# Adding a mixing bias to x on VectorE instead of through four small-K TensorE products a group

## What is computed

```python
att   = softmax(mlp(cond_128))                      # 64 x 8
agg_w = einsum('bk,koi->boi', att, weight)          # a 32x32 channel mixer per batch
agg_b = att @ bias_k                                # 64 x 32: one number per batch and channel
m     = einsum('boi,bih->boh', agg_w, x) + agg_b[:, :, None]
gate  = top-2 softmax over 8 experts of m @ gate_w.T
x1    = x + m @ base_w.T + base_b + 2.0 * (lora experts of m, weighted by gate)
out   = x1 + second layer (9-tap grouped convolution of x1, top-2 of 4 lora experts)
```

## Time and profile before

| | |
|---|---|
| median of 3 runs | 185.46 us (184.99 to 186.48) |
| profiled execution, its device time | 185.67 us |
| profiled execution, its span | 183.7 us |
| busy over the span | PE 96%, DVE 65%, POOL 46%, ACT 45% |
| granted TensorE clock | 1.0 in the mean |

### The profile page before, as it was taken

One profiled execution on the slowest core, in us unless ns is written; L12 is line 12 of the kernel. 1 busy time (PEld: TensorE's weight loads), 2 busy tenths in 40 slices (PEclk: granted clock), 3 DMA queues, 4 the chain that ended last, 5 costly groups with the idle time before them and its releaser, 6 DMA issues.

```text
span 183.7 us, 3003 instructions
## 1 busy us (share of the span) xinstructions
PE 176.0 (96%) x1087; PEld 160.1 (87%) x1087; DVE 119.6 (65%) x255; ACT 82.9 (45%) x183; POOL 84.2 (46%) x86
## 2 busy tenths in 40 slices
PE   7999999899999999999999999999999999988990
PEld 7998889788888999998889999988889999987970
DVE  1269795987996343987954336987756733577473
ACT  3656759538336066423442267316134652244010
POOL 8023609980396469930009099530007873433000
PEclk9999999999999999999999999999999999999999
DMA  5999000033000410000032000000140000000336
GB/s 176 312 373 366 11 0 2 4 109 121 0 0 25 149 60 0 4 0 0 0 133 99 0 2 0 4 0 0 61 167 4 2 0 4 0 0 2 114 114 228
DMA packets 6350, 12.15 MB, mean 66 GB/s; under 512 B 704, under 2 KB 1088, under 8 KB 6336
## 3 DMA queue, kind: packets, MB, share of 16 engines
q1 hardware_dynamic: 6192, 11.84, 18.1%
q10 hardware_dynamic: 144, 0.13, 0.3%
HBM read 7.77 MB, written 4.19 MB: 65 GB/s over the span
## 4 chain that ended last, share of the span: by engine, by line
PE 76%; DVE 16%; ACT 4%; issue 2%; DVEq 0%; POOL 0%; POOLq 0%
PE ps L895 17%; PE ps L897 17%; PE ps L896 17%; PE ps L917 6%; PE ps L971 5%; PE ps L888 3%; DVE xs L732 2%; DVE late L642 2%; DVE xsl L634 2%; PE ps L932 2%; DVE above L638 1%; PE ps L968 1%; PE ps L1060 1%; DVE outb L720 1%; PE ps L1079 1%
## 5 line engine op out<-in xcount | busy, mean ns | idle before, releaser
L895 PE MATMUL ps<-base_h,xTh 128*128 128x512 f32 x64 | 26.0, 406 | 0.0
L897 PE MATMUL ps<-base_h,xTl 128*128 128x512 f32 x64 | 25.2, 394 | 0.0
L896 PE MATMUL ps<-base_l,xTh 128*128 128x512 f32 x64 | 25.2, 394 | 0.0
L320 POOL TENSOR_TENSOR xTl<-xT_s,xTh 128x512 fp32r<-128x512 f32 x12 | 15.0, 1278 | 15.9 <-ACT xTh L404 15.9
L325 POOL TENSOR_TENSOR zl<-outb,zh 128x340 fp32r<-128x340 f32 x15 | 14.6, 976 | 13.4 <-ACT zh L429 13.3
L336 POOL TENSOR_TENSOR x1Tl<-x1T,x1Th 128x512 fp32r<-128x512 f32 x12 | 16.4, 1379 | 8.1 <-DVE lw L662 8.1
L691 DVE TENSOR_TENSOR outb<-ps,s_sb 128x340 f32<-128x340 f32 x16 | 8.2, 511 | 17.6 <-PE ps L897 11.2
L678 DVE SCALAR_TENSOR_TENSOR x1T<-ps,side_s,xT_s 128x512 f32<-128x512 f32 x16 | 12.0, 749 | 11.3 <-PE ps L897 11.3
L971 PEld LDWEIGHTS ps<-mixT,p 128*128 128x128 f32 x128 | 17.0, 191 | 1.4
L971 PE MATMUL ps<-mixT,p 128*128 128x128 f32 x128 | 17.0, 276 | 0.0
L429 ACT ACTIVATE zh<-outb 128x340 fp32r<-128x340 f32 x16 | 7.8, 489 | 17.9 <-DVE outb L691 13.2
(11 more groups left out here) (183 smaller groups left out, 471.5 us busy)
## 6 DMA issues: line engine op xcount, KB each, us to landing
xT_s<-in_xT_dram SPq DMA_DIRECT2D x16, 256.0 KB, 3.8
out_dram<-outb SPq DMA_DIRECT2D x16, 256.0 KB, 2.3
x1T<-in_wT_dram SPq DMA_DIRECT2D x4, 256.0 KB, 6.0
x1T<-in_az_dram SPq DMA_DIRECT2D x1, 680.0 KB, 8.3
...
```

The source lines that it names most:

```text
L320: nc.gpsimd.tensor_tensor(xTl[:, c, :], xT_s[:, g % 2, c, :], xTh[:, c, :].bitcast(F32), ALU.subtract).then_inc(x_lo, 1)
L895: nc.tensor.matmul(dst, sh, mh, start=start and c == 0, stop=False)
L896: nc.tensor.matmul(dst, sh, ml, start=False, stop=False)
L897: last = nc.tensor.matmul(dst, sl, mh, start=False, stop=stop and c == n - 1)
```

## The change

The bias no longer goes into bank Y[c]. Its parts are:

1. A bias row per group: `bias_row(i)`, one matmul of a matrix of ones (40 x 128) by row_b (40 x 512), writes the bias of each token to all partitions of bank 6 (BROW). It stands in `make_y` behind the mixer products of chunk 0 and waits for `lwT_lo` (bank 6 held the transposed lw) and `obc_lo`. The four products at L968 go; the first mixer product of a chunk now starts the bank.
2. Column sums as a column: row_w becomes one partition in plain fp32; four fp32 products with one column each (WSUM, bank 1) turn it into sum_w, 128 x 4, copied by DVE. They stand behind `x_base(0)` on PE. The subtraction for the low part of row_w goes.
3. `bias_x(i, c)` on DVE: xT_s = bias row * sum_w[:, c] + xT_s, in place, ahead of each `make_x1(i, c)`, which waits for it. It waits for the bias row and for the readers of xT_s (`x_lo`, `xl_mm`). `mix_logits` of the next group waits for all four `bias_x` (`xb_ok`), since it writes bank 6.
4. row_b loses its copy in partitions 64 to 71 (one ScalarE copy a group), and `bias_high(g)` waits for the bias row of group g-1 instead of the whole of `make_y`.
5. Order: the four `mix_half` move from among `make_x1(0, c)` to behind `route0(1)`, and `lwT_low(1)` ahead of the sums of group 0. On ACT `mix_place(2)` and `mix_place(3)` move behind `sums_high(0, 3)`, and `sums_high(0, 0..1)` behind `p0_out(1, 3)`. On POOL `context(0)` moves behind `x_low(2, c)`. On PE `mix_logits(1)` moves ahead of the products for pj_sum, which now use bank 1 instead of 7 and wait for x1_ok of all four chunks.

```diff
-KB = 64 + K0
+KB = 32 + K0
...
-        row_w = sb("row_w", [P, D], F32R)
-        row_b = sb("row_b", [96, TOK], F32R)
+        row_w = sb("row_w", [1, D])
+        sum_w = sb("sum_w", [P, DC])
+        row_b = sb("row_b", [KB, TOK], F32R)
...
-        HID, ATT, LGS, BSUM = 7, 6, 5, 1
+        HID, ATT, LGS, BSUM, WSUM, BROW = 7, 6, 5, 1, 1, 6
-        psum_b = ps[:, 7, 0:PJ]
+        psum_b = ps[:, 1, 0:PJ]
...
-            context(0)
             for i in range(1, G):
                     for c in range(DC):
                         x_low(n, c)
+                    if i == 1:
+                        context(0)
...
             def bias_high(g):
-                    act.wait_ge(y_mm, DC * g)
-                for r in (0, 64):
-                    nc.scalar.activation(row_b[r:r + K0, :], xs_flat[0:K0, :], ACT.Copy).then_inc(obc_hi, 1)
+                    act.wait_ge(brow_mm, g)
+                nc.scalar.activation(row_b[0:K0, :], xs_flat[0:K0, :], ACT.Copy).then_inc(obc_hi, 1)
-            for g in range(1, G):
-                mix_place(g)
+            mix_place(1)
             bias_high(1)
-            sums_high(0, 0)
-            sums_high(0, 1)
             p0_out(1, 2)
             lwT_high(1)
             p0_out(1, 3)
-            sums_high(0, 2)
-            sums_high(0, 3)
+            for t in range(TG):
+                sums_high(0, t)
+            mix_place(2)
+            mix_place(3)
...
+            def bias_x(i, c):
+                dve.wait_ge(brow_mm, i + 1)
+                dve.wait_ge(xT_in[i % 2][c], 16 * (i // 2 + 1))
+                dve.wait_ge(x_lo, DC * i + c + 1)
+                dve.wait_ge(xl_mm, 2 * (i + 1))
+                nc.vector.scalar_tensor_tensor(out=xT_s[:, i % 2, c, :], in0=ps[:, BROW, :], scalar=sum_w[:, c:c + 1],
+                                               in1=xT_s[:, i % 2, c, :], op0=ALU.mult, op1=ALU.add).then_inc(xb_ok, 1)
             def make_x1(i, c):
+                bias_x(i, c)
                 dve.wait_ge(y_mm, DC * i + c + 1)
+                dve.wait_ge(xb_ok, DC * i + c + 1)
-            dve.wait_ge(bsum_hi, 1)
-            minus(row_w[64:96, :], ps[64:96, BSUM, :], row_w[64:96, :]).then_inc(bsum_lo, 1)
+            dve.wait_ge(wsum_mm, 1)
+            nc.vector.tensor_copy(sum_w[:, :], ps[:, WSUM, 0:DC]).then_inc(wsum_ok, 1)
...
             def mix_logits(i, t):
                 if i and t == 0:
-                    pe.wait_ge(lwT_lo, i)
+                    pe.wait_ge(xb_ok, DC * i)
             def mix_base(i, c):
-                nc.tensor.matmul(ps[:, Y[c], :], row_w[0:KB, cols(c)], row_b[0:KB, :], start=True, stop=False)
                 for t in range(TG):
                     pe.wait_ge(p0_ok, TG * i + t + 1)
-                    nc.tensor.matmul(ps[:, Y[c], cols(t)], p0[:, t, cols(c)], mixer(i, t), start=False, stop=False)
+                    nc.tensor.matmul(ps[:, Y[c], cols(t)], p0[:, t, cols(c)], mixer(i, t), start=t == 0, stop=False)
+            def bias_row(i):
+                pe.wait_ge(lwT_lo, i + 1)
+                pe.wait_ge(obc_lo, i + 1)
+                nc.tensor.matmul(ps[:, BROW, :], ones_r[0:KB, :], row_b[:, :], start=True, stop=True).then_inc(brow_mm, 1)
             def make_y(i):
                 for c in range(DC):
                     mix_base(i, c)
+                    if c == 0:
+                        bias_row(i)
                     experts0(i, c)
...
+            pe.wait_ge(bsum_ok, 1)
+            for c in range(DC):
+                last = nc.tensor.matmul(ps[:, WSUM, c:c + 1], row_w[0:1, cols(c)], ones[0:1, 0:1], start=True, stop=True)
+            last.then_inc(wsum_mm, 1)
             turn_lw(0)
```

More of the change, by code:

```diff
@@ L520, in _ @@
             act.wait_ge(bsum_mm, 1)
-            nc.scalar.activation(row_w[:, :], ps[:, BSUM, :], ACT.Copy).then_inc(bsum_hi, 1)
+            nc.scalar.activation(row_w[:, :], ps[0:1, BSUM, :], ACT.Copy).then_inc(bsum_ok, 1)
             act.wait_ge(in_tap, 16)
@@ L810, in _ @@
             route0(1)
+            for g in (2, 3):
+                for half in range(2):
+                    mix_half(g, half)
+            dve.wait_ge(agg_ok, MIX_STEPS[G - 1])
+            lwT_low(1)
             sums(0, 0)
@@ L816, in _ @@
             sums(0, 3)
-            lwT_low(1)
             sums_low(0, 2)
@@ L1113, in _ @@
                     x_base(0, t, (c,))
+            pe.wait_ge(bsum_ok, 1)
+            for c in range(DC):
+                last = nc.tensor.matmul(ps[:, WSUM, c:c + 1], row_w[0:1, cols(c)], ones[0:1, 0:1], start=True, stop=True)
+            last.then_inc(wsum_mm, 1)
             turn_lw(0)
             x_logits(1, 0)
[L1116 removed]
+            pe.wait_ge(wsum_ok, 1)
             x_logits(1, 1)
             make_y(0)
+            for t in range(TG):
+                mix_logits(1, t)
             pe.wait_ge(in_az, 16)
[L1120 removed]
+            pe.wait_ge(x1_ok, DC)
             for m in range(2):
@@ L1125, in _ @@
             last.then_inc(pjsum_mm, 1)
-            for t in range(TG):
-                mix_logits(1, t)
             x_base(1, 0)
```

35 lines of the change are left out of this document (12 added, 23 removed).

## The result

The changed kernel takes **187.16 us** (median of 6 runs, 186.61 to 188.79), the kernel before 185.65 us (6 runs, 184.99 to 186.57). The ratio is 1.012, 95% interval 1.0076 to 1.0163: about 2.2 us slower, where the two medians lie 1.5 us apart. Ratios in this document leave out executions that took over 1.5% longer than the fastest of the same kernel. I had forecast no change, 185.6 us.

A forecast was written before the change was run, and what follows sets the result against it. PE, busy 96% of the span, was taken as the bound, with DVE's chain full before group 1's first x1. +1.1 us (groups 0, 1) and -0.9 (groups 2, 3) gave +0.2, forecast 185.6 us from the runs' median 185.46; range 183.4 to 187.6.

The forecast's parts named there:

- Four rows a group become one, K = 40 instead of 72. I give it the same 0.23 us: PE, make_y: one bias row replaces four bias products a group at 0.23 us each; alone 2.8 us less.
- my sum: Whole kernel: +1.1 us in groups 0 and 1, -0.9 in groups 2 and 3, together +0.2 us.
- the wait for ACT's last p0: Groups 2 and 3, chunk 0: mixer products wait 0.2 us for ACT's copy; net gain 0.47 us a group.
- I price that at nothing, and at 0.6 us if it doesn't: Group 3: DVE runs some 0.6 us later against PE and catches up in project(2); cost nothing, otherwise 0.6 us.
- the slow sums of group 0: DVE, before group 1's x1: sums at 0.93 us beside POOL's x1_low(0) would take 0.42 us with POOL idle.
- The term of the column products: PE behind x_base(0): four fp32 one-column products, eight passes, add 0.8 us; bounds 0 and 2.2 us.
- the stall in group 1: make_y(1), chunk 2: PE waits 1.7 us for DVE's first x1, where it waited 0.22; make_y(1) ends at 63.5 to 63.6.
- 5.8 us of mixers put into a chain that was full: DVE, group 1: four mix_half of 1.45 us each moved ahead of lwT_low(1); an argument against the full saving.
- no cost elsewhere: Other edits: ACT's later high parts and POOL's later x_low(2) stay hidden; 1 us before taps(0) if cover were gone.
- The rival of a slow exchange: Group 1: DVE's exchange with ACT takes 1 to 2 us more than counted; 186.6 to 187.6 us, chance 0.11.
- The upper end of my range: Whole kernel: 187.6 us, taking in the milder slow case and leaving out the fully slow exchange.
- the rival of the full saving: No new group 1 stall: -2.0 us, 183.5 us, or -1.6, 183.9 us, with 0.2 us waits; chance 0.22.

The follow-up runs named there:

- run 1: Changed kernel with the bias row over 72 partitions (32 more rows of zeros) instead of 40: ratio 1.0039 to the kernel before, PE distance 151.46 us.
- run 3: Changed kernel with the bias row at K = 64 instead of 40: ratio 1.0129 to the kernel before, PE distance 152.38 us.
- run 4: Changed kernel without the sixteen bias_x on DVE, everything on PE kept: ratio 1.0052 to the kernel before, PE distance 151.34 us.
- run 9: Changed kernel with a 72-row bias row and z_full(2, 0) ahead of sums_low(3, 0) on DVE: ratio 1.0049 to the kernel before.
- run 11: Changed kernel with 72-row bias row placed before mixer tile 3, group 1 and 3 reorders, and column products at K = 128: 184.10 us, ratio 0.9937.
- run 6: Changed kernel with the four mix_half back among make_x1(0, c): 191.61 us, ratio 1.0357 to the kernel before.
- run 7: Changed kernel with mix_half back among make_x1(0, c), group 0 sums ahead of lwT_low(1), sums_high(0, 0..1) ahead of p0_out(1, 2): ratio 1.0271.
- run 8: Changed kernel with a 72-row bias row, group 1's make_x1 between group 0's sums, x_high(2) ahead of mix_place(2) and (3): ratio 1.0031.
- run 10: Changed kernel with 72-row bias row, placed between mixer products of tiles 2 and 3, plus DVE/ACT reorders in groups 1 and 3: 184.46 us, 0.9941.

## Why the prediction was wrong

**The first step that failed: "Four rows a group become one, K = 40 instead of 72. I give it the same 0.23 us".** The change shrank the contraction from 72 rows to 40, and I took fewer rows to cost no more. Between products of 128 rows a product of 40 or 64 rows costs 0.41 us a group more than one of 72 (runs 1 and 3; 0.31 in group 0). In `make_y` this is 1.13 us (0.31 + 0.41 + 0.41; group 1 is bound by DVE either way), of which 0.18 us comes back before `project(3, 0)`, where PE then waits longer for DVE: 0.94 us in the distance (run 1), of the 2.2 us by which the distance missed my sum. With 72 rows groups 2 and 3 gain 0.48 and 0.50 us against before, and I had said 0.47: the rest of that step's working, the wait for ACT's last p0 included, was right. In group 0 the 72 rows give 0.37 of the 0.55 us that I had forecast up to `x_base(1)`; the other 0.18 stays open.

**The second: DVE's lateness in group 3, "I price that at nothing, and at 0.6 us if it doesn't".** It was 0.69 us. I reckoned how late `bias_x` makes DVE (0.6 us; 0.87 came) and not what else changes there: its sum and low part, 0.71 and 0.68 us before, now meet a POOL instruction that has already started and take 1.04 and 1.78. Runs 4 and 9 each bring `z_full(2, 0)` back into the time that PE can bear, run 4 by the 0.87 us of `bias_x`, with the slow sum and low part still there, run 9 by putting the instruction that PE waits for first. Either of the two causes alone would have been hidden. I had used the slow sums of group 0 (0.93 against 0.42 us) for a gain there, and didn't ask where else the two engines would meet.

**The term of the column products was undersized.** "I take 0.8 us"; 0.98 came, and 0.08 more ahead of the first. With 128 rows they take 0.81 (run 11), so the nearest row that I used was right for its own row count, and I missed a second time that few rows can cost more. Whether the step of these products lies at 64 rows too, no run shows.

**Right: the stall in group 1, in size.** Mixers undisturbed at 5.75 us (forecast 5.8), sums at 0.42, `bias_x` at 744 ns, a chunk at 1.58 to 1.60 us where nothing waits, `make_y(1)` 0.89 us longer for 0.82, the idle time 1.18 us for 1.7. That it ends at 63.15 for 63.5 to 63.6 is luck: the program's start was 1.19 us shorter in this profile, and against the end of `x_base(0)` all of group 1 comes 0.8 us later than I had it, by what group 0 and the column products had lost. The 0.5 us less of idle time is largely the dear bias row, which took it from PE: with 72 rows it is 1.59. But my reason for it, "5.8 us of mixers put into a chain that was full", is not how it works. In the changed kernel the chain that ends last in group 1 runs from `turn_lw(1)` through lwT_low and the sums behind it (DVE even waits 0.85 us ahead of lwT_low); taking the mixers out of the time before it changes nothing (run 6), taking the sums from behind lwT_low does (run 7). Where DVE has no room for the mixers is group 0: put back there, they cost 3.3 us (run 6).

**Right: no cost elsewhere.** PE has no gap in `taps(0)`, and all other stages are within 0.06 us of before. The rival of a slow exchange (186.6 to 187.6 us) gives the time that was measured, but not by its mechanism: the sums of group 0 were fast. The upper end of my range came from that rival, so that 187.16 us lies inside it is luck as well. Of the rival of the full saving, 1.6 to 2.0 us, run 11 gets 1.04 in the distance: groups 2 and 3 give the 0.7 us each, group 0 gives 0.46 up to `x_base(1)`, and group 1 gives nothing, with two waits for x1 of 0.39 and 0.33 us left in `make_y(1)`.

From the changed kernel to run 11 the distance falls by 3.45 us, which is so divided if the gains of runs 8 and 9 add: 0.94 for the 72 rows (run 1), 0.81 for the order in group 1 (run 8), 0.87 for the order in group 3 (run 9), 0.18 for the column products (run 11), and the remaining 0.65 for the bias row's place in the wait for p0 (run 10, 151.46 - 0.81 - 0.87 - 149.13), 0.24 of it in each of groups 2 and 3.
